# First graph layer: the search for the maxima split into two pairs of heads, the second pair three tiles behind

## What is computed

```
h = (layer_norm(x) @ W1).reshape(n, 4, 192)
s_src = (h * a_src).sum(-1);  s_dst = (h * a_dst).sum(-1)
e = leaky_relu(s_src[src] + s_dst[dst], 0.2)
emax = segment_max(e, dst);  ee = exp(e - emax[dst])
alpha = ee / segment_sum(ee, dst)[dst]
out = segment_sum(alpha[:, :, None] * h[src], dst)
```

## Time and profile before

| | us |
|---|---|
| median of 3 runs | 1964.48 |
| lowest, highest | 1963.42, 1965.52 |
| the profiled execution's own time | 1960.23 |
| span of its trace | 1958.4 |
| PE, DVE, ACT busy | 1789.6, 1546.7, 725.7 |

### The profile page before, as it was taken

One profiled execution on the slowest core, in us unless ns is written; L12 is line 12 of the kernel. 1 busy time (PEld: TensorE's weight loads), 2 busy tenths in 40 slices (PEclk: granted clock), 3 DMA queues, 4 the chain that ended last, 5 costly groups with the idle time before them and its releaser, 6 DMA issues. The chain is left out here.

```text
span 1958.4 us, 24113 instructions
## 1 busy us (share of the span) xinstructions
PE 1789.6 (91%) x8406; PEld 1339.3 (68%) x8407; DVE 1546.7 (79%) x2925; ACT 725.7 (37%) x1245; POOL 19.4 (1%) x38
## 2 busy tenths in 40 slices
PE   5679987499999899999699999997999979999997
PEld 3435544399954455555599999997899965555554
DVE  7869868799667663999699999996656638988996
ACT  5768966544214221111344444442321212322331
POOL 0000001010000000000000000000000000000000
PEclk9989998799999999999899999998999989999999
DMA  6200029642171326453221212111166557777764
GB/s 166 79 5 26 31 92 369 242 127 59 39 222 42 129 85 243 140 202 106 99 85 58 85 58 84 58 58 37 57 215 203 156 181 264 236 237 248 248 215 166
DMA packets 163159, 266.82 MB, mean 136 GB/s; under 512 B 11263, under 2 KB 131830, under 8 KB 160090
## 3 DMA queue, kind: packets, MB, share of 16 engines
q1 hardware_dynamic: 109434, 201.41, 31.3%
q10 hardware_dynamic: 50336, 49.66, 7.8%
q0 software_dynamic: 3264, 14.16, 2.0%
HBM read 209.48 MB, written 55.71 MB: 135 GB/s over the span
## 5 line engine op out<-in xcount | busy, mean ns | idle before, releaser
L1261 PE MATMUL ps<-work 128*128 128x193 f32 (+1 forms) x3200 | 530.8, 330 | 32.6 <-DVE work L2163 32.6
L1261 PEld LDWEIGHTS ps<-work 128*128 128x128 f32 x3200 | 530.3, 191 | 33.7 <-issue 33.7
L1284 PE MATMUL ps<-work 128*128 128x384 f32 (+1 forms) x1050 | 341.8, 488 | 11.2 <-DVE work L2264 11.2
L1675 ACT ACTIVATE work<-work,s 128x1280 f32<-128x1280 f32 x160 | 217.9, 1363 | 293.3 <-DVE work L2157 293.3
L1284 PEld LDWEIGHTS ps<-work 128*128 128x128 f32 x1050 | 200.0, 191 | 152.7 <-issue 13.7
L2157 DVE SCALAR_TENSOR_TENSOR work<-work,sd 128x1280 f32<-128x1280 f32 x160 | 247.6, 1548 | 38.6 <-PE ps L1261 25.7
L1215 PE MATMUL ps<-work 128*128 128x384 f32 (+1 forms) x720 | 237.0, 490 | 3.1 <-ACT work L1565 2.6
L2163 DVE SCALAR_TENSOR_TENSOR work<-work,counts 128x1280 f32<-128x1280 f32 x160 | 237.5, 1485 | 2.7 <-ACT work L1675 2.6
L1215 PEld LDWEIGHTS ps<-work 128*128 128x128 f32 x720 | 136.3, 190 | 100.4 <-issue 15.3
L1825 DVE TENSOR_SCALAR work<-work,winoff 125x480 bf16<-125x480 f16 x480 | 157.7, 397 | 0.4 <-issue 0.3
L1695 ACT ACTIVATE work<-work,s 128x256 f32<-128x256 f32 x150 | 68.0, 500 | 223.3 <-DVE work L2237 223.2
(11 more groups left out here) (268 smaller groups left out, 1936.8 us busy)
## 6 DMA issues: line engine op xcount, KB each, us to landing
work<-hs_d SPq DMA_DIRECT2D x75, 960.0 KB, 5.4
work<-pqrow_d SPq DMA_DIRECT2D x18, 1280.0 KB, 6.4
nomask_d<-work SPq DMA_DIRECT2D x40, 320.0 KB, 6.9
work<-nomask_d SPq DMA_DIRECT2D x40, 320.0 KB, 3.1
hx_d<-work ACTq DMA_DIRECT2D x60, 192.0 KB, 1.9
work<-hx_d SPq DMA_DIRECT2D x120, 96.0 KB, 1.9
hs_d<-feat ACTq DMA_DIRECT2D x22, 480.0 KB, 3.6
feat<-srow_d SPq DMA_DIRECT2D x3, 2560.0 KB, 12.7
```

The costliest lines, as they stand in the source:

```text
L1261: last = mm(sums_at(c, t, u), xe[i % RING][:, t * P:(t + 1) * P], hx[:, i % RING, 0:1 + c.width], start=(r == 0 and k == 0 and t % TB == 0 ...
L1284: last = mm(bank(product_bank(g, i), width), a[:, at * P:(at + 1) * P], h[:, block_, 0:width], start=(m == 0), stop=(m == STEPS_D - 1), sk ...
L1675: nc.scalar.activation(xe[i % RING][:, 0:n_], xe[i % RING][:, 0:n_], ACT.Exp, bias=s02[:, k, bass.ds(rh, 1)], scale=0.8).then_inc(s.exp_do ...
```

## The change

The four heads of layer a's search become two pairs.

- The scores of the heads 0 and 1 are loaded before the sixteenth store of a projected tile, those of the heads 2 and 3 where the whole load stood. The projection's weights move so that the first half of `sbc_wide[0]` is free by then.
- In step t DVE makes the same masks, then searches tile t for the first pair and tile t - 3 for the second. Three further steps hold only searches of the second pair.
- The total masks have five buffers of their own, the others a ring of five. A total's buffer is written again when the second pair's search of five tiles before is done.
- `rows_of_maxima` works on a pair. That of the first stands in step 9 between the two searches; its rows are turned, copied, written and loaded (buffer `pqb_a[0]`) ahead of the barrier. That of the second stands in phase 1 after the weights of step 1. PE turns its rows before step 2, ACT copies them after the exponential of step 4, SP writes them before the load of step 7.
- For this, layer a's pair rows and weights change places in memory (`pqb_a`, `xe_a`).

The diff, cut to its core:

```diff
+MASK_RING, MASKS_OUT, TOTALS, LAG = 3, 5, 5, 3
+S_ROWS_AT, S_LOAD_AT = 12, 15
+PAIR_TURN_AT, PAIR_COPY_AT, PAIR_OUT_AT = 2, 4, 7
...
+MAX_A = [th for step in range(T + LAG) for th in [*((step, h) for h in range(2) if step < T),
+                                                  *((step - LAG, h) for h in range(2, 4) if step >= LAG)]]
+MAX_A_AT = {th: i + 1 for i, th in enumerate(MAX_A)}
...
+            def a_scores_load(p):
+                sp.dma_start(sbc_wide[0][:, 2 * p:2 * p + 2, :].rearrange("p h n -> p (h n)"),
+                             srow_d[2 * p:2 * p + 2, :].rearrange("h n -> (h n)").partition_broadcast(P)).then_inc(s.s_in[p].sem, 16)
             for n in range(2 * T):
...
+                if n == S_LOAD_AT:
+                    sp.wait_ge(sa_out, 16)
+                    a_scores_load(0)
                 sp.wait_ge(*s.proj_ev.at(n + 1))
...
-            sp.wait_ge(sa_out, 16)
-            sp.dma_start(sbc_wide[0].rearrange("p h n -> p (h n)"),
-                         srow_d[0:A.RH, :].rearrange("h n -> (h n)").partition_broadcast(P)).then_inc(s.s_in[0].sem, 16)
+            a_scores_load(1)
...
             sp.wait_ge(pq_c, 1)
+            sp.dma_start(pqrow_d[0:4, :], pair_rows[0][0:4, :]).then_inc(pq_out, 16)
             sp.wait_ge(pq_out, 16)
+            sp.wait_ge(v_done, 11)
+            sp.dma_start(pqb_a[0], pqrow_d[0:2, :].partition_broadcast(P)).then_inc(s.pq_in[0].sem, 16)
...
                 act.wait_ge(nm_turned, n + 1)
+                to, uses, landed = mask_out(n)
+                if uses:
+                    act.wait_ge(*landed.at(16 * uses))
+                    if r == TOTAL:
+                        act.wait_ge(*s.max_done.at(MAX_A_AT[t - TOTALS, 3]))
...
+            def search_a(t, p):
+                for h in (2 * p, 2 * p + 1):
+                    i = MAX_A.index((t, h))
                     if i >= 2:
                         dve.wait_ge(*s.max_done.at(i - 1))
+                    v.tensor_tensor_reduce(junk_a[i % 2], sbc_wide[0][:, h, :], nm_total[t % TOTALS], 1.0, -3.0e38,
                                            ALU.subtract, ALU.max, mx[:, t, h:h + 1]).then_inc(s.max_done.sem, 1)
+            def searches_a(rows_of_maxima):
+                no_edges(0)
+                for t in range(T + LAG):
+                    if t < T:
+                        for n in range(4 * t + 1, min(4 * t + 5, 4 * T)):
+                            no_edges(n)
+                        dve.wait_ge(nm_copied, 4 * t + 1)
+                        if t == 0:
+                            dve.wait_ge(*s.s_in[0].at(16))
+                        search_a(t, 0)
+                    if t == T - 1:
+                        rows_of_maxima(0)
+                    if t >= LAG:
+                        if t == LAG:
+                            dve.wait_ge(*s.s_in[1].at(16))
+                        search_a(t - LAG, 1)
...
@@ in phase 1: SP, PE, ACT, DVE @@
+                                if c is A and i == PAIR_OUT_AT:
+                                    sp.wait_ge(pq_c, 2)
+                                    sp.dma_start(pqrow_d[4:8, :], pair_rows[1][0:4, :]).then_inc(pq_out, 16)
...
+                            if c is A and i == PAIR_TURN_AT:
+                                pe.wait_ge(pq_ready, 2)
+                                turn_pair(1)
+                            if c is A and i == T:
+                                pe.wait_ge(pq_c, 2)
...
+                            if c is A and i == PAIR_COPY_AT:
+                                copy_pair(1)
...
+                            if c is A and i == 1:
+                                rows_of_maxima(1)
```

More of the change, by code:

```diff
@@ L395, in gnn_program, with __init__, at @@
         hx_a = carve(work, (RING + 4) * NP, RING * H2C).rearrange("p (s c) -> p s c", s=RING)
-        assert (RING + 4) * NP + RING * 769 <= 16648
+        pqb_a = [carve(work, 2 * i * NP, 2 * NP).rearrange("p (c n) -> p c n", c=2) for i in range(2)]
+        xe_a = [carve(work, (4 + i) * NP, NP) for i in range(RING)]
+        assert (RING + 4) * NP + RING * H2C <= 12512 and 12512 + NP <= 16648 - DT * 384
+        xe_of = lambda c: xe_a if c is A else xe
+        pqb_of = lambda c: pqb_a if c is A else pqb
+        assert (RING + 4) * NP + RING * 769 <= 16648
+        class Signal:
+            def __init__(self, sem_, before):
+                self.sem, self.before = sem_, before
+            def at(self, n):
+                return self.sem, n + self.before
         phase = sem("phase")
@@ L431, in gnn_program @@
         bias_in, ones = sem("bias_in"), sem("ones")
[L433 to L440, removed]
         class Shared:
@@ L1012, in _, with turn_pair @@
             pe.wait_ge(pq_ready, 1)
[L1013 to L1016, removed]
+            def turn_pair(p):
+                for t in range(T):
+                    last = nc.tensor.transpose(ps[0:4, 5 * 512 + t * P:5 * 512 + (t + 1) * P], pq[:, t, 4 * p:4 * p + 4], identf[:, :])
+                last.then_inc(pq_t, 1)
+            turn_pair(0)
             end_phase(pe, 0)
@@ L1443, in _, with copy_pair @@
                     nc.scalar.activation(to, own[:, :, q], ACT.Copy).then_inc(v_saved, 1)
-            act.wait_ge(pq_t, 1)
-            nc.scalar.activation(rows_a[0:2 * A.RH, :], ps[0:2 * A.RH, 5 * 512:5 * 512 + NP], ACT.Copy).then_inc(pq_c, 1)
+            def copy_pair(p):
+                act.wait_ge(pq_t, p + 1)
+                nc.scalar.activation(pair_rows[p][0:4, :], ps[0:4, 5 * 512:5 * 512 + NP], ACT.Copy).then_inc(pq_c, 1)
+            for i in range(3):
+                act.wait_ge(*s.hx_out[i].at(16 * ring_share(2 * T, i, 3)))
+            copy_pair(0)
             end_phase(act, 0)
@@ L2129, in layer @@
-                if c is DD:
+                    for r in range(R):
+                        last = v.tensor_tensor(pqv[:, :, r, :, 0], pqv[:, :, r, :, 1], d_[:, :, r, :], ALU.add)
+                    last.then_inc(pq_ready, 1)
+                if c is A:
+                    searches_a(rows_of_maxima)
+                elif c is DD:
                     project_d(ci, s, rows_of_maxima)
@@ L2170, in normalise @@
                     return v.tensor_scalar(o, z_ap, 1.0e-30, None, ALU.max)
-                return exponents, weights, normalise
+                return exponents, weights, normalise, rows_of_maxima
             def attention(ci, c, ph):
@@ L2179, in attention @@
                     return
-                exponents, weights, normalise = layer(ci, c, ph)
+                exponents, weights, normalise, rows_of_maxima = layer(ci, c, ph)
                 if c is not DD:
```

139 lines of the change are left out of this document (72 added, 67 removed).

## The result

The changed kernel takes 1957.1 us, the median of 6 runs (1954.3 to 1958.9), against 1963.95 for the kernel before (6 runs): ratio 0.9968, interval [0.9954, 0.9981]. The shift of 6.9 us was forecast as 7.5 and the time as 1957.0.

The account below looks back on a forecast made before the run. It took DVE to set the pace of layer a's search, with PE's long run behind it. -8.5 (E), -0.3 (behind E) and +1.3 (turning) gave -7.5 us: 1957.0 from the median 1964.48, range 1950.5 to 1963.5.

Parts of the forecast that it names:

- The release by the weights piece: Start of layer a's search: PE's weights piece, not the scores, releases it; little of DVE's 11.6 us idleness is used.
- W: Layer a's search: landing of PE's first weights piece, forecast at 294.1 us, 3.3 us earlier.
- The chain after W: Layer a's masks: PE and ACT pace the first steps, then DVE at 7.37 us each; E at W + 70.8.
- E: End of the first pair rows' small operations on DVE, forecast at W + 70.8 = 364.9 us, 8.5 us earlier.
- Behind E: Before the attention: the pair rows' landing at E + 12.2 decides, not the eight searches and barrier at E + 11.8.
- F-E: From E to the start of PE's long run: forecast 18.1 us and not 18.4, so -0.3.
- Inside the attention: In PE's long run: turning the second pair's rows adds 1.3 us; the additions on DVE, ACT and SP cost nothing.
- The sum: Whole kernel: -8.5, -0.3 and +1.3 give -7.5 us; a shift of one stage holds in profiled time and median.
- (a): Layer a's search: weights land no earlier, or DMA engines bind the early chain; -4.2 to -2.5 us; chance 0.18.
- (b): Layer a's search: DVE's waits for masks nearly vanish, E at W + 67.4; -10.9 us, 1953.6; chance 0.12.
- (c): Mask chain: PE's clock falls to half more often; five slow rounds beyond three give +6.5 us, 1971; chance 0.08.
- (d): Behind E: the second pair's eight searches stand on the way in full; +3.8 us, 1968; chance 0.05.

Follow-up runs that it names:

- e2: Changed kernel, but the first pair's scores are loaded after the last projected tile, like the second pair's; 1961.5 us, 0.9991 of the kernel before.
- e5: Changed kernel, lag of three tiles kept, with the first pair's small operations moved behind the last search; 1968.1 us, 1.0029 of the kernel before.
- e3: Changed kernel with the second pair's scores loaded later, after the sixth mask's store; 1959.0 us, 0.9978 of the kernel before.
- e9: e3 with nine of twelve weights loads left out, PE reading the first three pieces again; first weights load's issue to PE's long run 96.6 us.
- e6: Changed kernel with a lag of 0 tiles and the first pair's small operations behind the last search; 1961.6 us, 0.9991 of the kernel before.
- e1: Changed kernel with a lag of 0 tiles instead of three, the early load kept; 1958.6 us, 0.9975 of the kernel before.

## Why the prediction was right

**The release by the weights piece.** It held. DVE made two searches and mask 5, then idled until PE had turned mask 3. e2 shows the other side: with the scores late, only W mattered. W came 3.2 us earlier by the means (14.5 to 11.3), forecast 3.3. Two values in that walk were off and made up for each other: the two queues moved 0.35 MB/us and not 0.38 (1.76 MB from 289 to 294 us, and the earlier trace rows give no more), and the weights had 35% of it (0.61 MB) and not 31%. That the early load itself costs nothing held as well (45.7 us, above).

**The chain after W.** Walked from W, the searches of the tiles 1, 2 and 3 were to start at 6.15, 13.6 and 19.2; the trace has 302.72, 310.52 and 315.98 less 296.69, that is 6.0, 13.8 and 19.3. Step 9 was to begin its searches at 63.0 plus 3.4 of waits; it did at 65.7. E was forecast at W + 70.8 and stood at 70.1 and 69.6. DVE's later waits for masks were 2.5 us in the first trace, below the 3.4 kept. By the means E-W fell by 6.0 us, forecast 5.2.

**Behind E.** Here the decider was the other one. The prediction let the landing of the pair rows decide at E + 12.2. The issue of that load and what it took, SP's timeline and the DMA issues (KB, us to landing) of the changed kernel:

```profile
371.92 0.33 SPq L613 DMA_DIRECT2D work<-pqrow_d  x1
```
```profile
work<-pqrow_d SPq DMA_DIRECT2D x1, 1280.0 KB, 5.9
```

It was down at 377.8, E + 11.0, and the last search and the barrier ended at 378.5. Of the 1.2 us by which the landing came sooner than forecast, 0.7 lie before the issue (E + 5.1, forecast 5.8) and 0.5 in the load. DVE started at E + 11.8, the value worked out for that branch, and F-E fell by 0.7 and not 0.3. That the eight searches are worth their full 11.3 us there is shown by e5 (110.7 against 98.9, 11.8). The Trainium skill ("DMA: Bandwidth & Descriptors", Anatomy of one DMA) gives 2.0 us and the bytes over 436 GB/s, fitted on the software queue; for this load, which is on the hardware queue, that is an estimate of 5.0 us. It took 5.9 with no other transfer of size beside it, so the 6.4 was nearer, though the branch that the page's figure would have picked is the one that came.

**Inside the attention.** The turning took 1.25 us (forecast 1.3), PE never idled between F and G, yet the run with it, from F to G, is only 0.6 us longer by the means. The three traces of before differ by as much among themselves (136.2 to 136.8), so the missing 0.7 has no cause shown.

**The sum, and the step that failed.** Sum of the stage: 9.2 us, forecast 7.5. The forecast undersized E-W by 0.8, F-E by 0.4 and took 0.7 too much for the turning. The last step, that a shift of one stage holds to the end, failed: by the traces 2.9 us were lost again in C-G. The two misses stand against each other, so the closeness of 1957.1 to 1957.0 is in part luck. The forecast of a gain near 7 us was right in its mechanism, with these two sizes off.

**The rivals.** (a) did not occur as put, since W moved; its collision on the DMA engines is real, as e3 and e9 show, but cost ACT only 2.0 us here. (b) did not occur: the stage's gain of 9.2 lies as far from its 10.9 as from the forecast's 7.5, but the waits for masks in the later steps did not vanish (2.5 us). (c), a slower mask chain by the clock, did not happen in the stage (three row pieces took 2.78 us, as before); an earlier fall of the clock did go with a loss of 3 us, in another stage. (d) is refuted by F-E (17.7) and e5.

**What the parts are worth.** Of the 9.8 us of F-S, the early load gives about 4 (e2; with the halved rows 3.7 in e6), the forming of the first pair's rows ahead of the last two searches 3 to 5 (e1 against e6), and the lag of three tiles the last 1 to 3 (e1 against the changed kernel), which single traces hardly tell from nothing. The lag moves six more searches behind E, but it takes them out of steps in which DVE then waits for PE.

## What to carry to other kernels

An idle engine that waits for one transfer may stand, a few instructions later, behind a second one: find the next release before counting the idle time as gain. Work that is moved out of a chain pays only if the engine has something else to do there; count its waits in the emptied steps. When two kernels differ by a few microseconds, take marks by stage in several traces of each: here one pair of spans differed by 1.5 us, the stage by 9.2 and the medians by 6.9. An experiment that comes out at the forecast sum can still have two terms wrong: compare term by term, as in e2.

## What the runs showed of the hardware

- Here two queues shared the DMA engines packet by packet, not byte by byte: 57 against 60 packets with 20 KB and 4.7 KB, 102 against 108 with 10 KB and 4.6 KB. With the shorter row the other queue moved 0.50 MB in 4 us and not 0.28. The Trainium skill ("DMA: Bandwidth & Descriptors", Queues, rings and completion order) speaks of turns by packet, which agrees, and of packets of several descriptors; the records here bear out no more than one row against one.
- A broadcast load of 1280 KB took 5.9 us alone (changed kernel) and 12.0 among masks and weights (e3).
- With the fall of PE's clock one gap earlier the first four tiles of the third layer took 30.1 to 32.9 us and not 28.4 to 29.2, in all eleven traces with the change against three without, though the code of these tiles is the same. Its cause is open.
